# First FFN product of a gated attention block for four tiles per matmul (512 tokens) in place of two (256)

## What is computed

```python
x = x + jnp.tanh(g_xattn[0]) * _L0_xattn_ref(_layernorm(x, axis=-1), ctx_1024, ctx_1024)
x = x + jnp.tanh(g_ffn[0]) * _L0_ffn_ref(_layernorm(x, axis=-1), ...)
# _L0_xattn_ref: scores of 16 heads of width 16, causal mask, softmax, attn @ v
# _L0_ffn_ref:
prob = jax.nn.softmax(xf @ w_router + b_router, axis=-1)
_, idx = jax.lax.top_k(prob, TOP_K)                       # 4 of 16 blocks
h = jax.nn.relu(jnp.einsum('nd,ebd->neb', xf, w1b) + b1b[None])
y = jnp.einsum('neb,ebd,ne->nd', h, w2b, mask) + b2[None, :]
```

## Time and profile before

| | |
|---|---|
| device time, median of 3 runs (all) | 693.99 us (693.48, 693.99, 698.29) |
| profiled execution: span from first to last instruction | 694.6 us |
| PE busy | 671.8 us, 97% of the span |
| POOL / DVE / ACT busy | 564.2 / 519.7 / 511.9 us |
| mean granted clock of PE | 0.993 of full speed |

### The profile page before, as it was taken

One profiled execution on the slowest core, in us unless ns is written; L12 is line 12 of the kernel. 1 busy time (PEld: TensorE's weight loads), 2 busy tenths in 40 slices (PEclk: granted clock), 3 DMA queues, 4 the chain that ended last, 5 costly groups with the idle time before them and its releaser, 6 DMA issues.

```text
span 694.6 us, 30557 instructions
## 1 busy us (share of the span) xinstructions
PE 671.8 (97%) x13072; PEld 623.5 (90%) x13072; DVE 519.7 (75%) x1429; ACT 511.9 (74%) x785; POOL 564.2 (81%) x778
## 2 busy tenths in 40 slices
PE   6779999999999999999999999999999999999998
PEld 5668899999999999999989999999999999999997
DVE  6788877877777787787787787778777777877752
ACT  3657787787787878778778777877877877786642
POOL 5687889889888888988988988898898888886642
PEclk9989999999999999999999999999999999999999
DMA  5322345444335354344444444533533544342010
GB/s 162 95 78 39 83 114 75 106 113 80 95 101 110 86 99 113 79 82 113 113 79 103 105 72 99 114 95 86 113 83 82 110 113 77 75 83 50 20 38 32
DMA packets 161814, 61.90 MB, mean 89 GB/s; under 512 B 135696, under 2 KB 161424, under 8 KB 161680
## 3 DMA queue, kind: packets, MB, share of 16 engines
q1 hardware_dynamic: 160848, 58.38, 37.7%
q10 hardware_dynamic: 832, 1.57, 0.8%
HBM read 19.03 MB, written 8.39 MB: 39 GB/s over the span
## 4 chain that ended last, share of the span: by engine, by line
PE 87%; DVE 4%; POOL 3%; SPq 2%; DMA 1%; issue 1%; ACT 1%; POOLq 0%; DVEq 0%
PE bank L411 10%; PE score_banks L332 10%; PE score_banks L302 8%; PE bank L413 8%; PE bank L412 8%; PE bank L436 8%; PE bank L435 8%; PE bank L434 8%; PE bank L345 8%; PE bank L359 4%; PE bank L370 3%; PE bank L381 1%; PE score_banks L315 1%; DMA qT<-qT 1%; PE bank L389 1%
## 5 line engine op out<-in xcount | busy, mean ns | idle before, releaser
L837 POOL TENSOR_TENSOR h_low<-hid,h_high 128x512 fp32r<-128x512 f32 x128 | 164.8, 1287 | 12.8 <-ACT hid L535 12.6
L709 DVE SCALAR_TENSOR_TENSOR hid<-bank,b_cols,used_all 128x256 f32<-128x256 f32 x248 | 108.2, 478 | 73.0 <-PE bank L413 66.9
L513 ACT ACTIVATE weights<-score_banks 128x1024 f32<-128x1024 f32 x128 | 124.3, 1023 | 40.3 <-PE score_banks L332 40.3
L411 PE MATMUL bank<-xT_high,w_high 128*128 128x256 f32 x496 | 150.7, 304 | 0.3 <-DVE hid L709 0.2
L830 POOL TENSOR_SCALAR_AFFINE_SELECT weights<-weights 128x1024 f32<-128x1024 f32 x128 | 138.3, 1105 | 8.6 <-ACT weights L513 8.2
L413 PE MATMUL bank<-xT_high,w_low 128*128 128x256 f32 x496 | 139.2, 281 | 0.0
L412 PE MATMUL bank<-xT_low,w_high 128*128 128x256 f32 x496 | 139.1, 280 | 0.0
L434 PE MATMUL bank<-w_high,h_high 128*128 128x256 f32 x488 | 137.3, 281 | 0.7 <-POOL h_low L837 0.7
L436 PE MATMUL bank<-w_high,h_low 128*128 128x256 f32 x488 | 138.0, 283 | 0.0
L435 PE MATMUL bank<-w_low,h_high 128*128 128x256 f32 x488 | 137.5, 282 | 0.0
L794 POOL TENSOR_SCALAR ve<-mv 128x1 f32<-128x1 f32 x128 | 34.6, 271 | 89.9 <-DVE mv L620 89.8
(11 more groups left out here) (102 smaller groups left out, 1508.4 us busy)
## 6 DMA issues: line engine op xcount, KB each, us to landing
x_in<-in_x SPq DMA_DIRECT2D x31, 256.0 KB, 3.3
out_y<-y_out SPq DMA_DIRECT2D x31, 256.0 KB, 2.4
c_in<-in_ctx SPq DMA_DIRECT2D x30, 256.0 KB
qT<-qT SPq DMA_DIRECT2D x128, 4.0 KB
w_stage<-in_w1T ACTq DMA_DIRECT2D x1, 1024.0 KB, 5.9
hid<-in_w2T SPq DMA_DIRECT2D x8, 128.0 KB, 2.7
kT_parts<-k_parts SPq DMA_TRANSPOSE x57, 2.8
qT_parts<-q_parts SPq DMA_TRANSPOSE x57, 2.7
```

The source lines that it names most:

```text
L411: pe.matmul(out=bank, lhsT=w1_high[:, k, c], rhs=high, start=k == 0, stop=False)
L513: act.activation(weights[:, b % 2, half * 2 * HB:(half + 1) * 2 * HB, :].rearrange("p h q -> p (h q)"), score_banks[:, 2 * half:2 * half + ...
L709: dve.scalar_tensor_tensor(hid[:, n % 4, j], hid_bank(n)[:, j * TOKS:(j + 1) * TOKS], b1_cols[:, c:c + 1], used_all[:, p % 2], ALU.add, AL ...
L837: pool.tensor_tensor(h_low[:, p % 2, chunks], hid[:, n % 4], h_high[:, p % 2, chunks].bitcast(F32), ALU.subtract).then_inc(h_low_made, 1)
```

## The change

Tiles are grouped in units. The first two units are pairs as before (tiles 0 to 3); from tile 4 on a unit is four tiles, and `hidden` streams the 512 tokens of the unit in one matmul: a piece is then one chunk, 1 x 2 x 3 = 6 matmuls with 512 columns, and fills one bank as before. A unit of four has eight pieces, two to a turn, made four turns long, at a lag of 7 turns (QUAD_LAG) in place of 5; its tiles leave through `ffn_out` at a lag of 11 (QUAD_OUT_LAG) in place of 7. `ffn_out` itself keeps its 24 matmuls for a tile. DVE handles a piece in one instruction of 512 elements in place of two of 256. The loop ends four turns later. For memory, the attention weights and `oT` have one buffer in place of two, the staging of w1 lies in the slots of `x2_b2` that are used late, and `h_high` and `h_low` are made of 26 cells (128 tokens x 2 chunks), which a unit of four reuses in mirrored order as the cells of the unit before come free.

```diff
--- before.py
+++ after.py
@@ constants
+QUAD = 4
+PAIR_UNITS = 2
+QUAD_LAG = 7
+QUAD_OUT_LAG = 11
@@ buffers
-        w1_stage = sb("w1_stage", [P, KC, BLOCKS, HC, UNITS], F32)
-        XS, CS, QS, VS, TS, GS = 12, 4, 2, 5, 3, 8
+        XS, CS, QS, VS, TS, GS = 12, 4, 2, 5, 3, 11
-        weights = sb("weights", [P, 2, HEADS, S], F32)
-        oT = sb("oT", [P, 2, BANK], F32)
+        weights = sb("weights", [P, HEADS, S], F32)
+        oT = sb("oT", [P, BANK], F32)
+        STAGE_SLOT = GS - KC * HID // D
+        w1_stage = x2_b2[:, STAGE_SLOT:GS].rearrange("p g n -> p (g n)").rearrange(
+            "p (k e c r) -> p k e c r", k=KC, e=BLOCKS, c=HC)
-        xT_high = sb("xT_high", [P, 2, KC, PAIR, S], F32R)
-        xT_low = sb("xT_low", [P, 2, KC, PAIR, S], F32R)
+        xT_high = sb("xT_high", [P, 2, KC, QUAD, S], F32R)
+        xT_low = sb("xT_low", [P, 2, KC, QUAD, S], F32R)
-        used_all = sb("used_all", [P, 2, TOKS], BF16)
-        hid = sb("hid", [P, 4, PC, TOKS], F32)
-        h_high = sb("h_high", [P, 2, HC, TOKS], F32R)
-        h_low = sb("h_low", [P, 2, HC, TOKS], F32R)
+        used_all = sb("used_all", [P, 2, QUAD, S], BF16)
+        hid = sb("hid", [P, 4, PIECE], F32)
+        CELL_OF = [sum(2 * QUAD - j for j in range(k)) for k in range(HC // 2)]
+        CELLS = CELL_OF[-1] + 2 * QUAD - (HC // 2 - 1)
+        h_high = sb("h_high", [P, CELLS, 2, S], F32R)
+        h_low = sb("h_low", [P, CELLS, 2, S], F32R)
@@ which tile belongs to which unit, and when
+        def unit_of(b):
+            return b // PAIR if b < PAIR_UNITS * PAIR else PAIR_UNITS + (b - PAIR_UNITS * PAIR) // QUAD
+        def cell(u, k):
+            if u < PAIR_UNITS:
+                return CELL_OF[k] + u * (QUAD - 1)
+            return CELL_OF[k] + (0 if mirrored(u) else QUAD - k)
-        def hidden_pair(i):
-            p, half = divmod(i - FFN_LAG, 2)
-            return (p, 2 * half) if 0 <= p < PAIRS else (None, None)
+        def hidden_unit(i):
+            for first, last, lag in ((0, PAIR_UNITS * PAIR, FFN_LAG), (PAIR_UNITS * PAIR, N, QUAD_LAG)):
+                if first <= i - lag < last:
+                    u = unit_of(i - lag)
+                    return u, 2 * (i - lag - first_of(u))
+            return None, None
         def out_tile(i):
-            return i - OUT_LAG if 0 <= i - OUT_LAG < N else None
+            if 0 <= i - OUT_LAG < PAIR_UNITS * PAIR:
+                return i - OUT_LAG
+            return i - QUAD_OUT_LAG if PAIR_UNITS * PAIR <= i - QUAD_OUT_LAG < N else None
-        FIRST, LAST = -4, N - 1 + OUT_LAG + 1
+        FIRST, LAST = -4, N - 1 + QUAD_OUT_LAG + 1
@@ hidden (TensorE); u is the unit, m the piece in it
-                for j in range(PC):
-                    c = PC * m + j
-                    bank = hid_bank(n)[:, j * TOKS:(j + 1) * TOKS]
+                toks = tiles_in(u) * S
+                for j in range(PIECE // toks):
+                    c = m * (PIECE // toks) + j
+                    bank = hid_bank(n)[:, j * toks:(j + 1) * toks]
                     for k in range(KC):
-                        high, low = (t[:, ps, k].rearrange("p t s -> p (t s)") for t in (xT_high, xT_low))
+                        high, low = (t[:, slot, k].rearrange("p t s -> p (t s)")[:, 0:toks] for t in (xT_high, xT_low))
@@ ffn_out (TensorE)
-                if t == 0:
-                    pe.wait_ge(h_low_made, PIECES * p + 2 * half + 2)
+                if b == first_of(u):
+                    pe.wait_ge(h_low_made, first_piece(u) + (half + 1) * pieces_in(u) // 2)
-                    high, low = h_high[:, p % 2, c, toks], h_low[:, p % 2, c, toks]
+                    at = cell(u, c // 2) + position(b)
+                    high, low = h_high[:, at, c % 2], h_low[:, at, c % 2]
@@ hidden_masked (VectorE)
-                for j in range(PC):
-                    c = PC * m + j
-                    dve.scalar_tensor_tensor(hid[:, n % 4, j], hid_bank(n)[:, j * TOKS:(j + 1) * TOKS],
-                                             b1_cols[:, c:c + 1], used_all[:, p % 2], ALU.add, ALU.mult
-                                             ).then_inc(hid_made, 1)
+                for j in range(PIECE // toks):
+                    c = m * (PIECE // toks) + j
+                    part = slice(j * toks, (j + 1) * toks)
+                    masked = dve.scalar_tensor_tensor(hid[:, n % 4, part], hid_bank(n)[:, part], b1_cols[:, c:c + 1], mask,
+                                                      ALU.add, ALU.mult)
+                masked.then_inc(hid_made, 1)
@@ hidden_low (GpSimd)
-                pool.tensor_tensor(h_low[:, p % 2, chunks], hid[:, n % 4], h_high[:, p % 2, chunks].bitcast(F32),
+                pool.tensor_tensor(hidden_place(h_low, u, m), hidden_of(hid, n, u), hidden_place(h_high, u, m).bitcast(F32),
                                    ALU.subtract).then_inc(h_low_made, 1)
@@ GpSimd, before x2_b2 is written
+                    if b == STAGE_SLOT:
+                        pool.wait_ge(w_high_made, 4)
+                        pool.wait_ge(w_low_also_made, 2)
```

171 lines of the change are left out of this document (99 added, 72 removed).

## The result

| | before | after |
|---|---|---|
| device time, median (lowest to highest), 4 runs each on one chip | 694.58 us (693.48 to 698.29) | 702.99 us (701.16 to 703.98) |
| ratio, 95% interval | | 1.0115 (1.009 to 1.014) |
| profiled execution, span | 694.6 us | 702.2 us |

The change makes the kernel 1.15% slower by the ratio, 8.4 us between the medians, where 5.5 us less were forecast. Wherever the record has both, an execution's device time is 1.7 to 2.3 us longer than its span, so the two may not be set equal as was done ahead of the prediction. The profiled execution before, with its span of 694.6 us, was rather one of some 696.5 us, which may be why the spans lie only 7.6 us apart.

A forecast was written before the change was run, and what follows sets the result against it. PE, busy 97% of the span, was taken to bound the kernel. 694.0 - 15.0 (width) + 9.2 (idle) + 0.5 (late landings) - 0.1 = 688.6, stated as 688.5 us; 8 in 10 range 683.5 to 695.5.

The forecast's parts named there:

- part 1: 512 columns for 256 in `hidden`: step 0.2155 us, 0.125 us less a piece, 15.0 us less PE work over 120 pieces.
- rival A: `hidden` matmuls: the 0.011 us of each step does not hide; 8.4 us gained in place of 15.0, 695.2 us; chance 0.12.
- other bound: `hidden` at 512 columns: 0.011 us paid per matmul, step 0.2247 us, a piece 1.348 us, 0.070 us less.
- rival E: `hidden` matmuls: step grows with the columns, 0.236 us at 512; no width gain, 9.2 us idle, 703.5 us; chance 0.02.
- Three groups: Matmuls L359, L345, L332: steps 0.108, 0.104, 0.114 us, weight loads 142, 110, 188 ns; taken to show the load sets the step.
- Part 2: Larger lags leave holes in front and add turns behind: PE idles 9.2 us together; 16.5 us more work behind the last tile.
- s9 to s15: The hole: `shifted_scores` of tile 9 to that of tile 15; six intervals forecast at 52.4 us, PE needing 44.6, idle 7.8.
- no limit: DVE in the hole: `out_transposed` to the end of `row_maximum` 4.6 us, plus half a turn of 3.0, 7.7 us.
- Part 3: Buffers, cells, waits and DVE's single instruction: no wait added by single buffers; a few late landings in full turns cost 0.5 us.
- B: Hole costs little, POOL and the route carry their slack through: 4 us idle in place of 9.2, 683.3 to 685; chance 0.25.
- C: Hole gives nothing back: landing before `shifted_scores` holds intervals at 10.2 us, PE idles 18.1 us, 697.6 us; chance 0.08.
- D: PE's clock falls in the hole: 2.7 us for each fall, 691.2 us, or 694 for two; chance 0.13.

The follow-up runs named there:

- short trains: Kernel without the computation: six fp32r matmuls of 512 columns, or twelve of 256, behind four transposes; a train took 1.48 us or 1.52 us.
- long rows: Kernel without the computation: rows of 24 matmuls of one kind, other engines silent, then busy; fp32r settled at 0.2267 us (512 columns) and 0.1200 (256).
- units-last kernel: Changed kernel with 30 pairs ahead of its units of four in place of two, so only the last four tiles form such a unit: 703.2 us, ratio 1.0117.
- the filler: Changed kernel with twelve more PE transposes into a free bank ahead of `shifted_scores` in turns 9 to 14: 704.7 us, ratio 1.0112.

## Why the prediction was wrong

**The step that failed** is the one of part 1 at 512 columns: "0.2133 + about 0.002 = 0.2155 us", with the weight load as the cause of the 0.011 us at 256. In its place the runs showed 0.233 to 0.234 us in the changed kernel and with the width alone, and 0.231 in the short trains. A piece gains 12 x 0.118 - 6 x 0.2335 = 0.015 us by its steps and (10.215 - 10.165) / 2 = 0.025 by the full turns; with the 2.5 us measured for the width alone, 0.021. Forecast was 0.125, so for 120 pieces 2.5 us in place of 15.0. This is 12.5 of the 14.5 us between forecast and result. The weight load was half right at 256 columns, where short loads take 6.7 of the 13.3 ns away, and wrong at 512, where they take nothing. The gain was lost in two parts. The surcharge is paid per matmul and doesn't hide (rival A's mechanism): from 0.125 to 0.056 by the settled steps. And a train of six at 512 columns doesn't reach the settled step: from 0.056 to 0.02. (With 0.120, the settled step at 256, the first would be 0.080: the kernel's twelve are a little quicker than a settled row, its six slower.) My "other bound", 0.2247, bounded nothing, since it took the surcharge of a train of twelve at 256 for that of one of six at 512. In place it is 0.011 at 256 and 0.020 at 512, as if it grew with the columns, which is rival E's result without its mechanism.

**The misreading.** Three groups lay in the order of their weight loads, and I took the load as the cause. L359, the row that decided, is a transpose, 128 f32 columns that I read as 256 fp32r columns; it says nothing on how fast fp32r streams. None of the three groups had the type and the columns of `hidden`, and they differed in the rows of the array and in how many ran at once besides the load; only the load stood in my table. The row that could decide, a train of fp32r with more than 256 columns, was not in the trace of before. All other outcomes of an unmeasured step had 0.14 together, on the strength of an analogy.

**The Trainium skill** ("TensorE: Matmul & The Clock Gate", "Back-to-back issue gap") has N/2.4 + 2.5 ns for a single matmul at full clock, from which the forecast worked out 701.5 us; measured 702.99. For bf16 the runs agree: 215.8 and 109.1 ns at 512 and 256 columns. For fp32r they don't: 226.7 and 120.0 in long rows, and 228 to 236 in trains of six. That its sum came within 1.5 us is chance in the size of the surcharge: with 2.5 ns a matmul there is little to save, and here there were 13, of which the short trains took most back. At half the clock its N/1.2 agrees with 427 ns.

**Part 2, the moved work,** was right in kind and nearly in size. From s9 to s15 PE's work at full clock is 45.5 us (an estimate: the forecast's 44.6, with nine pieces 0.10 dearer each), so 9.3 us are lost there where 7.8 was forecast; the nine pieces' price makes the rest of the distance from 52.4 to 54.8. Not all of the 9.3 is idle time: by the row PE is busy 47.65 and idle 7.1, and the slow clock in one interval takes 1.7. The intervals are 8.05, 8.97, 8.90, 9.76, 9.35 and 9.76 us, for a forecast of 7.8, 8.6 and four of 9.0. Forecast was one limit, POOL with the landing. Measured are two by turns, the landing (5.5 us in 4 waits) and DVE's maxima (2.6 in 3). Of POOL's part the trace shows this much: in both intervals of 9.76 us POOL is busy 9.59, over the 95% that the forecast named as its sign, and in the others 6.4 to 8.1. The forecast's route had SP's queue in it only as the time of one `max_row`; the chain above has 6.4 us of it. DVE had "no limit" in the forecast, from rows of full turns. In the hole some of its operations take longer. The timeline of the changed kernel, DVE and POOL:

```profile
119.26 1.63 DVE L719 SCALAR_TENSOR_TENSOR x<-att,tanh_g,x_in 128x256 f32<-128x256 f32 x1
119.31 1.29 POOL L895 TENSOR_TENSOR h_low<-hid,h_high 128x512 fp32r<-128x512 f32 x1
```

This is `attention_added`, 1.63 us beside `hidden_low`, where its median is 0.52. Four of its six instances in the hole take 0.99 to 1.63, and all operations that are longer there than their medians add up to 4.1 us of DVE (0.9 in the same stretch before). They lie on the route to the maxima; how much of the 9.3 us is theirs is not shown, since no run took them away alone.

**Ahead of s9** 1.2 us were lost where nothing was forecast. All of it is there by s1 (26.03 against 24.80): 0.6 at s0, which the change hardly touches and which stands at 16.66 to 18.16 in the runs here, and 0.65 from s0 to s1, where the mean clock was 0.79 in the profiled execution and 1.00 before. From 7.5 us to s0 it was 0.51, and 0.83 before. So this part is the state of the clock in two single executions, not shown to be the change's. `shifted_scores` of tile 62 stands 8.0 us earlier than before (630.52 against 638.51), for a forecast of 21, which had the wide pieces' gain in it. **Behind the last tile** 15.7 us were added, for a forecast of 16.5. **Part 3** held: `hidden_low` with its strided cells takes 1.29 us as before, the single buffers cost nothing (the units-last kernel's 55 turns), and DVE's one instruction of 512 elements takes 0.75 us in place of 0.87 for the two. The last term of the forecast's sum, 0.1 less, has no working there.

**The rivals.** A had the mechanism of the long rows, and the step too short for this kernel's trains. B (hole under 49 us) and C (over 58) did not come about in any form of the changed kernel but the one with POOL's order changed. D came about in the profiled execution: one interval at a clock of 0.82, worth 1.7 us of full-speed work by its row. PE was idle for only 0.4 us of it, but at full clock the interval would have been little shorter (8.99 with the filler). Where the clock fell behind the hole instead, it cost 1.5 us. E had 703.5 us by a step of 0.236 and an idle of 9.2 us; measured 702.99, by 0.234 and 9.3 lost. It had a chance of 0.02. "Grows with the columns" is its reading of two points in the kernel; the long rows, with 384 between them, show a fixed sum and a start that doesn't settle.

**Open.** What each interval of the hole would take without SP's queue, without DVE's longer operations or with a shorter queue on POOL has not been separated: the remedies for POOL and SP put a cost elsewhere, and the clock fell at different places in each profiled execution, so that stretches of single executions can be compared to within 1 or 2 us only. No version that does the whole computation beat the kernel before. The width by itself gains 0.5%, but four tiles to a unit need the lags, which cost over three times that by the ratios, and nearly five by the medians.

## What to carry to other kernels

Before trading instruction count for width, measure the step at the new width in a row of its own, in the operand type that the kernel uses: a kernel of 130 us decides it. Measure it in trains as long as the kernel's, too: fewer matmuls save only what is paid per matmul, and a shorter train may give that back. And a longer lag is not free because work is conserved: the turns that lose the work shrink only as far as the next limit lets them (here 6.5 of some 15.8 us), wherever in the program the hole is put, while the same work stands whole behind the last tile.
